# Reordering the fillers of the attention pipeline, and one buffer for two statistics

## The reference

```python
x = x + 0.5 * ffn(layernorm(x))      # shared SwiGLU + one of 8 routed experts per token
x = x + attention(layernorm(x))      # Nystrom attention, 16 heads of 16, 64 landmarks
x = x + 0.5 * ffn(layernorm(x))
```

```python
q_l, k_l = means of q, k over groups of 8 tokens         # 64 landmarks
s1 = softmax(q @ k_l.T); s2 = softmax(q_l @ k_l.T); s3 = softmax(q_l @ k.T)
z = s2.T / (max column sum * max row sum)
for _ in range(6):
    xz = s2 @ z
    z = 0.25 * z @ (13 I - xz @ (15 I - xz @ (7 I - xz)))
out = (s1 @ (z @ (s3 @ v))) @ Wo + bo
```

## Time and profile before

| | us |
|---|---|
| median of 3 runs | 1283.79 |
| lowest, highest | 1281.41, 1285.84 |
| profiled execution, its own time | 1283.79 |
| profiled execution, its span | 1281.9 |
| start of `chain_first(b, 0)` in periods 3, 4, 5, 6 | 627.38, 682.36, 737.35, 792.06 |

### The profile page before, as it was taken

One profiled execution on the slowest core, in us unless ns is written; L12 is line 12 of the kernel. 1 busy time (PEld: TensorE's weight loads), 2 busy tenths in 40 slices (PEclk: granted clock), 3 DMA queues, 4 the chain that ended last, 5 costly groups with the idle time before them and its releaser, 6 DMA issues.

```text
span 1281.9 us, 28898 instructions
## 1 busy us (share of the span) xinstructions
PE 1176.8 (92%) x10692; PEld 923.2 (72%) x10693; DVE 708.9 (55%) x1387; ACT 559.7 (44%) x887; POOL 539.8 (42%) x603
## 2 busy tenths in 40 slices
PE   4899999999995789999999999986899998999997
PEld 2688877888884456667676676764688887888886
DVE  7533236776663464656757557553642235666664
ACT  2422126666662445445354453421522224666663
POOL 0388205677773122322313231220168503766675
PEclk9899999999998799999999999997799999999999
DMA  8311523222111200000000000000611513222220
GB/s 327 149 50 50 193 77 108 64 68 74 59 61 53 83 2 3 2 3 2 3 2 2 2 2 2 3 2 1 269 44 50 188 37 115 64 65 63 68 70 21
DMA packets 41953, 80.16 MB, mean 63 GB/s; under 512 B 8948, under 2 KB 33655, under 8 KB 40832
## 3 DMA queue, kind: packets, MB, share of 16 engines
q1 hardware_dynamic: 28576, 53.54, 11.5%
q0 software_dynamic: 13280, 25.24, 6.5%
HBM read 57.17 MB, written 27.07 MB: 66 GB/s over the span
## 4 chain that ended last, share of the span: by engine, by line
PE 82%; DVE 11%; issue 4%; ACT 2%; DMA 1%; DVEq 0%; POOL 0%; POOLq 0%; ACTq 0%
PE PS L1396 17%; PE PS L1346 13%; PE PS L1410 10%; PE PS L1355 9%; PE PS L1576 4%; PE PS L1469 4%; PE PS L1589 4%; PE PS L1626 3%; PE PS L1403 3%; PE PS L1477 3%; DVE A_NM L653 2%; DVE A_NM L660 1%; PE PS L1385 1%; PE PS L1536 1%; PE PS L1511 1%
## 5 line engine op out<-in xcount | busy, mean ns | idle before, releaser
L1396 PE MATMUL PS<-WHL,XGH 128*128 128x512 f32 x624 | 217.9, 431 | 8.2 <-DVE XGL L566 4.5
L1228 POOL TENSOR_TENSOR A_A<-A_XC,A_ST 128x320 f32<-128x320 f32 (+1 forms) x96 | 72.9, 774 | 234.3 <-ACT A_ST L1020 234.2
L1410 PE MATMUL PS<-WD,XNT 128*128 x624 | 148.5, 381 | 1.5 <-ACT XNT L956 1.5
L1158 POOL DMA_INDIRECT X<-xs_dram,WHO x78 | 115.0, 1475 | 46.9 <-issue 46.9
L1396 PEld LDWEIGHTS PS<-WHL,XGH 128*128 128x128 f32 x624 | 111.7, 191 | 30.6 <-issue 7.9
L919 ACT ACTIVATE HSB<-PS 128x512 f32<-128x512 f32 x64 | 38.2, 597 | 216.3 <-PE PS L1346 216.3
L1164 POOL DMA_INDIRECT HSB<-shared_dram,WHO x78 | 81.1, 1040 | 114.7 <-DMA shared_dram<-X 91.4
L573 DVE TENSOR_TENSOR XNT<-XNT,PS 128x512 f32<-128x512 f32 x78 | 53.7, 688 | 135.0 <-PE PS L1396 135.0
L514 DVE TENSOR_TENSOR HB<-HSB,PS 128x512 f32<-128x512 f32 x64 | 44.0, 688 | 151.8 <-ACT HSB L919 151.8
L1396 PE MATMUL PS<-WHL,XGL 128*128 128x512 f32 x312 | 124.2, 398 | 0.0
L1410 PEld LDWEIGHTS PS<-WD,XNT 128*128 128x128 f32 x624 | 112.4, 190 | 14.5 <-issue 2.0
(11 more groups left out here) (205 smaller groups left out, 2323.4 us busy)
## 6 DMA issues: line engine op xcount, KB each, us to landing
WG<-in_r_gate SPq DMA_DIRECT2D x2, 4096.0 KB, 15.6
WU<-in_r_up SPq DMA_DIRECT2D x2, 4096.0 KB, 18.0
xs_dram<-X SPq DMA_DIRECT2D x16, 512.0 KB, 2.9
WD<-in_r_down SPq DMA_DIRECT2D x4, 2048.0 KB, 8.3
shared_dram<-X SPq DMA_DIRECT2D x16, 512.0 KB, 8.0
X<-in_x SPq DMA_DIRECT2D x4, 1024.0 KB, 9.2
X<-mid_dram SPq DMA_DIRECT2D x8, 512.0 KB, 3.8
X<-xs_dram,WHO POOLq DMA_INDIRECT x78, 3.4
```

Source lines behind the costliest of these rows:

```text
L1158: pool.indirect_dma_start(out=B["XS"][:, u * D:(u + 1) * D], out_offset=None, in_=xs_dram, in_offset=bass.IndirectOffsetOnAxis(ap=B["WHO"] ...
L1228: pool.tensor_tensor(a, x, st, ALU.add).then_inc(att["a"], 1)
L1396: ins = pe.matmul(banks[bank][:], tok, w[:, k * F:(k + 1) * F], start=(k == 0 and i == 0), stop=(k == KD - 1 and i == 2))
L1410: ins = pe.matmul(banks[7][:, 0:D], B["HT"][:, u * F + f * P:u * F + (f + 1) * P], B["WD"][:, bass.ds(ex * (KF * D) + f * D, D)], start=(f ...
```

## The change

Fillers move within the lists of the engines. The waits move with their fillers and stay what they were.

- TensorE: `s3_max(nxt, 1)` moves ahead of `denominators(old)` and `turn(far, 0)`. `turn_nm3(nxt)` moves ahead of `project_v(nxt, 0)`.
- VectorE: `chain_x(b, 1)` moves ahead of `project(done, 0)`. `batch_scale(ln)` moves from the fifth inverse step to behind `chain_x(b, 3)`.
- ScalarE: `rounded(nxt, 3)` moves ahead of `numerators(old)`. `batch_deviation(ln)` moves from behind `sums_kept(nxt, 1)` to between `exp3(nxt, 1)` and `exp1(b, 1)`.
- GpSimd: `batch_normalise(ln)` moves from the end of the period to between `chain_a(b, 3)` and `chain_a(b, 4)`. `add_bias` moves from the start of a period to the end of the one before.
- The buffer LNA goes; the layer norm of `ln` uses AGG, which `stats` of the finished batch overwrites later in the period.

```diff
-                           ("LNR", GT), ("LNM", GT), ("LNA", GT * 2), ("DSEL", PAIRS * (QUAD + 2)), ("BSEL", D)):
+                           ("LNR", GT), ("LNM", GT), ("DSEL", PAIRS * (QUAD + 2)), ("BSEL", D)):
...
-                    dve.bn_aggr(B["LNA"][:, j * 2:(j + 1) * 2], STATS[:, j * 6:(j + 1) * 6]).then_inc(res["agg"], 1)
+                    dve.bn_aggr(AGG[:, j * 2:(j + 1) * 2], STATS[:, j * 6:(j + 1) * 6]).then_inc(res["agg"], 1)
...
+                chain_x(b, 1)
                 if exists(done):
                     project(done, 0)
-                chain_x(b, 1)
...
                 chain_x(b, 3)
+                if exists(ln):
+                    batch_scale(ln)
...
                     column_max(nxt)
-                if exists(ln):
-                    batch_scale(ln)
...
                 chain_s(b, 0)
+                if exists(nxt):
+                    rounded(nxt, 3)
                 if exists(old):
                     numerators(old)
-                if exists(nxt):
-                    rounded(nxt, 3)
...
                     exp3(nxt, 1)
+                if exists(ln):
+                    batch_deviation(ln)
                 if exists(b):
                     exp1(b, 1)
                 chain_s(b, 4)
...
                     sums_kept(nxt, 1)
-                if exists(ln):
-                    batch_deviation(ln)
...
                 chain_a(b, 0)
-                if exists(far):
-                    add_bias(far)
...
                 chain_a(b, 3)
+                if exists(ln):
+                    batch_normalise(ln)
                 chain_a(b, 4)
...
                     weights_scaled(b)
                 if exists(ln):
-                    batch_normalise(ln)
+                    add_bias(ln)
...
                 chain_second(b, 0)
+                if exists(nxt):
+                    pe.wait_ge(att["qkr"], count("qkr", nxt, 4))
+                    pe.wait_ge(att["s3m"], count("s3m", nxt, 2))
+                    s3_max(nxt, 1)
                 if exists(old):
...
                     turn(far, 0)
-                if exists(nxt):
-                    pe.wait_ge(att["qkr"], count("qkr", nxt, 4))
-                    pe.wait_ge(att["s3m"], count("s3m", nxt, 2))
-                    s3_max(nxt, 1)
...
                 chain_second(b, 1)
                 if exists(nxt):
+                    pe.wait_ge(att["xo"], count("xo", done, 1))
+                    pe.wait_ge(att["xts"], count("xts", far, 1))
+                    pe.wait_ge(att["num"], count("num", old, 2))
+                    turn_nm3(nxt)
                     pe.wait_ge(att["xts"], count("xts", nxt, 2))
                     pe.wait_ge(att["xts"], count("xts", far, 2))
                     pe.wait_ge(att["rec"], count("rec", old, 1))
                     project_v(nxt, 0)
-                    pe.wait_ge(att["xo"], count("xo", done, 1))
-                    pe.wait_ge(att["xts"], count("xts", far, 1))
-                    pe.wait_ge(att["num"], count("num", old, 2))
-                    turn_nm3(nxt)
```

More of the change, by code:

```diff
@@ L624, in batch_scale @@
                 dve.wait_ge(res["rstd"], 2 * g + 1)
-                dve.scalar_tensor_tensor(B["LNM"][:], B["LNA"][:].rearrange("p (t c) -> p t c", c=2)[:, :, 0], -1.0, B["LNR"][:],
+                dve.scalar_tensor_tensor(B["LNM"][:], AGG[:].rearrange("p (t c) -> p t c", c=2)[:, :, 0], -1.0, B["LNR"][:],
                                          ALU.mult, ALU.mult).then_inc(res["rstd"], 1)
@@ L988, in batch_deviation @@
                 act.wait_ge(att["xn"], count("xn", g - 1, GT))
-                act.activation(B["LNR"][:], B["LNA"][:].rearrange("p (t c) -> p t c", c=2)[:, :, 1], ACT.Sqrt, bias=const("eps")).then_inc(res["sd"], 1)
+                act.activation(B["LNR"][:], AGG[:].rearrange("p (t c) -> p t c", c=2)[:, :, 1], ACT.Sqrt, bias=const("eps")).then_inc(res["sd"], 1)
             def turned(b, k):
@@ L1240, in attention_pool @@
             for b in PERIODS:
-                nxt, far, ln = b + 1, b + 2, b + 3
+                nxt, ln = b + 1, b + 3
                 chain_a(b, 0)
-                if exists(far):
-                    add_bias(far)
                 chain_a(b, 1)
```

## The result

The changed kernel takes 1299.57 us (median of 4 runs, 1299.05 to 1300.05); the kernel before took 1282.60 beside it (4 runs, 1281.39 to 1285.84). The ratio is 1.0128, with a 95% interval of 1.0109 to 1.0147: slower by 17.0 us, where 10.4 were forecast. The sign was right, the size was not, and 1299.57 lies 1.6 us above the top of the 80% range, 1298. Over twelve executions of the changed kernel the time runs from 1296.80 to 1308.23.

A forecast was written before the change was run, and what follows sets the result against it. TensorE, busy 52.25 of each 55.0 us period, was taken as the bound. Terms 8.6 + 1.4 + 2.9 - 1.7 - 0.8 = +10.4 on 1283.79 gave 1294.2 us, with an 80% range of 1290 to 1298.

The forecast's parts named there:

- The five stalls of the transpose: TensorE, periods 2 to 6: turn_nm3 waits for VectorE's later projection, chain_first(b, 2) 1.73 us late each time; +8.6 us.
- s3_max first: TensorE: s3_max waits 1.57 us, the 1.44 before s2_scores goes; +0.22 in periods 2 to 5, +0.55 in 1; +1.4 us.
- The Sqrt between the Exps: ScalarE: Sqrt and two table loads make exp1 late, 0.34 in periods 2 to 4, 1.30 in 0 and 1; +2.9 us.
- batch_scale's 0.29: VectorE, fifth step: batch_scale leaves the unbroken run, saving 0.29 us in each of periods -1 to 4; -1.7 us.
- The same two in period 1: Period 1: exp1 late by 1.30 us, less 0.29 for batch_scale out of the fifth step; 1.01 us.
- add_bias, the rounded copies and batch_normalise at nothing: GpSimd and ScalarE: these moves cost nothing; batch_normalise, its cover gone, would cost 11 us in five periods.
- no wait took up TensorE's loss: Rival: TensorE's lost time comes out of its 2.75 us of waiting per period; 1279.4 us, chance 4%.
- the load back did not wait: Rival, ScalarE: second table load waits with exp1, 1.28 us late in periods 2 to 4 too; 1297.0 us, chance 12%.
- no switch had a drain: Rival, ScalarE: a drain at both table switches in five periods gives about 13 us more; 1307 us, chance 2%.
- the sentence on batch_scale: VectorE: batch_scale's new place ahead of heads_norm delays nothing, as heads_norm waits for spread_denominators anyway; no cost.
- the term of the fill: Early periods: about -0.25 us in period -3, -0.5 in period -1 from the earlier transpose; -0.8 us.
- The clock: TensorE, periods 1 to 6: a lower clock named as a cost left out of the forecast; priced at nothing.

The follow-up runs named there:

- the two undoings: Changed kernel with project_v ahead of turn_nm3 on TensorE again (1292.87 us), or with project(done, 0) ahead of chain_x(b, 1) on VectorE again (1293.56 us).
- the kernel with the group back: Changed kernel with batch_scale, batch_deviation, batch_normalise and add_bias in their old places and LNA back; 1291.31 us, ratio 1.0052.
- the kernel that moves the group in period -1 alone: Kernel before with batch_scale, batch_deviation and batch_normalise in their new places in period -1 only; 1288.36 us, ratio 1.0045.
- one, shown above: Trace of the changed kernel with s3_max(nxt, 1) back behind denominators and turn(far, 0) on TensorE; 1297.15 us, ratio 1.0115.
- The kernel with the group back only up to period 1: Changed kernel with batch_scale, batch_deviation and batch_normalise in their old places in periods -3 to 1, LNA back; 1294.17 us, ratio 1.0085.
- The kernel with three moves: Kernel before with s3_max(nxt, 1) between denominators and turn, batch_scale behind product_kept, turn_nm3 ahead of project_v only without done; 1273.38 us, ratio 0.9936.

## Why the prediction was wrong in size

**What held.** The direction, and the mechanism in the full periods. The five stalls of the transpose: 1.63 a period in the two undoings, 1.73 forecast. s3_max first: 0.19, 0.22 forecast, with the stall moved from s2_scores to it. The Sqrt between the Exps, less batch_scale's 0.29: 0.10 (56.90 against 56.80 of the kernel with the group back), 0.05 forecast. The same two in period 1: 1.03, 1.01 forecast. The full period grew to 56.90, forecast 57.0. add_bias, the rounded copies and batch_normalise at nothing: nothing of them is seen in a full period; the early buffers were not tried by themselves. None of the rivals happened: no wait took up TensorE's loss, the load back did not wait, and no switch had a drain.

**The step that failed.** It is the sentence on batch_scale, "In its new place it stands ahead of heads_norm, which waits for spread_denominators, itself late by as much or more", and with it the term of the fill, -0.8, which holds nothing for this wait. That sentence is true of period 3, where I read it, and was then taken for six periods. In period -1 there are no denominators and no heads: what stands behind batch_scale on VectorE is row_max, which nothing holds back and for which TensorE waits. In its place stood a wait of 3.70 us more, shown by the kernel that moves the group in period -1 alone (+5.8 us, with the slow matmuls behind it) and by the one that moves batch_scale back (-4.5 us). I had gone through the fill for the transpose, where it gave a small gain, and not for each moved instruction that waits.

**What was left out.** The clock. The prediction named it as what would break it, and priced it at nothing. Behind the added waits in periods -1 and 1 TensorE works at 1.2 GHz for a stretch: L1469 3.62 us instead of 1.98 in period -1, the same matmuls 3.68 instead of 1.98 in period 1. TensorE in period 1 of the changed kernel:

```profile
560.80 0.73 PE L1618 MATMUL PS<-A_REC,A_BSEL 32*128 32x128 f32 x16 [1.99 <-issue]
561.53 3.68 PE L1469 MATMUL PS<-A_XTS,XNT 128*128 128x512 f32 x4
```

The wait ahead of L1618 is 1.99 us there and 0.64 in the kernel before. The Sqrt between the Exps, forecast at 1.30 for periods 0 and 1, thus lengthened it by 1.35. The slow matmuls behind it cost 1.70 more; of the six traces with this wait of 1.99 or 2.00 us, five have such a stretch behind it and one, shown above, has none.

**The account.** Measured 17.0, forecast 10.4. The group in period -1 by itself gives 5.8 (interval 3.6 to 8.1) where I had -0.29 for it. That is 6.1 of the 6.6 missed, but the agreement is better than its parts: it leaves no room for the clock in period 1, and periods 0, 1 and 6 vary from run to run with the clock. An estimate from the rows alone comes out near as well: 3.71 for the wait, 1.64 for the slow L1469 behind it, 0.29 for the saving that was counted there and 1.70 for the slow L1469 of period 1 make 7.3, and the periods 2 to 6 fell 0.5 short of their forecast together, which leaves 6.8. The kernel with the group back only up to period 1 did not come down as far as either account says. What is shown is that the group's move costs 8.5 to 9.8 us, that period -1 alone costs 3.6 to 8.1 of them, and that period 1 adds 1.03 by waiting in each trace and 1.7 by the clock in five of six. What stays open is when a stretch of the fill falls to the lower level.

## What to carry to other kernels

In a software pipeline written out by hand, a reorder is costed period by period in the fill and the drain too: for each moved instruction that waits, ask in each of them what is queued behind it once the usual neighbours don't exist. Moving the consumer ahead of its cover costs only if the producer moved back as well; undo either half. A piece that must come early goes behind the work that covers its inputs, not ahead of it, and in the thin periods of the fill a wait can cost more than its length, which no trace here shows for the full ones.

## What the runs showed of the hardware

The mean granted clock differs between runs of one kernel and goes with their times. The changed kernel: 0.970 in the runs of 1296.80 and 1297.05 us, 0.968 in those of 1299.04 to 1300.05, 0.967 at 1301.64, 0.966 at 1303.55, 0.963 at 1308.23, or about 1.6 us for each 0.001. The kernel with three moves: 1282.98 at 0.970 to 1270.08 at 0.981, about 1.2 for each 0.001. In the kernel before the order is looser: runs of 1282.95 and of 1286.91 us both have 0.971. So a comparison to 0.3% takes many runs, and part of a difference between two kernels can be how often a stretch falls to the lower level.

In the fill TensorE ran at 1.2 GHz after waits of 1.49 us (period 0, L1576 2.40 instead of 1.32), 1.99 us (period 1) and 4.42 us (period -1), while the waits of 1.49 and 1.59 us in period 3 left the clock at 1.00. The same waits of 1.49 us in period 0 and of 1.99 us in period 1 also stand in executions where the matmuls behind them ran at full clock. The Trainium skill, TensorE: Matmul & The Clock Gate, The HAM clock gate, says that TensorE works at 1.2 GHz after it has been idle and at 2.4 GHz once it has been busy; the row behind the 4.42 us agrees. That the same wait in the same place is followed by the lower level in one execution and by the higher in another is what the rows add.

Why the kernel with three moves has the higher clock in most of its runs is open: it has fewer waits, but no run here separates that.
